# The 144-wide block's seven steps spread among a 656-wide block's in the pairwise-tanh stage, and the filter schedule shifted to match

## What is computed

```python
def _L2_attn_ref(B, W, v):
    Wi = jnp.einsum('bnd,ed->bne', B, W)
    scores = jnp.einsum('d,bijd->bij', v, jnp.tanh(Wi[:, None, :, :] + Wi[:, :, None, :]))
    attn = jax.nn.softmax(scores, axis=-1)
    return jnp.einsum('bij,bjd->bid', attn, B)
...
t = _to_tokens(x)
t = t + _L2_attn_ref(_ln_t(t), L2_attn_W, L2_attn_v)
t = t + _L2_ffn_ref(_ln_t(t), ...)      # 8 experts, the best 2 of each token
t = t + _L3_attn_ref(_ln_t(t), ...)     # causal linear attention
t = t + _L3_ffn_ref(_ln_t(t), ...)      # 16 spectral filters (causal convolutions), then mixing matrices
```

## Time and profile before

| | us |
|---|---|
| median of 3 runs | 12501.48 |
| lowest, highest | 12500.0, 12501.75 |
| the profiled execution | 12500.22 |
| its span, first to last instruction | 12498.5 |
| its mean granted TensorE clock | 0.98 |
| span's part before the first pass | 6203.7 |

### The profile page before, as it was taken

The page is one execution under the profiler, slowest core; times in us unless marked ns, Lnnn a source line. Parts: engine busy times, 40 slices in busy tenths (PEclk is TensorE's granted clock), DMA queues, the critical chain, the costliest instruction groups (busy, mean ns, idle before and its releaser), DMA issues. The chain is left out here.

```text
span 12498.5 us, 297675 instructions
## 1 busy us (share of the span) xinstructions
PE 11704.8 (94%) x123040; PEld 5806.2 (46%) x123040; DVE 11385.2 (91%) x21539; ACT 10886.1 (87%) x7444; POOL 126.2 (1%) x103
## 2 busy tenths in 40 slices
PE   8999999999999999999867999999999999999999
PEld 3333333333333333333323555555555555555567
DVE  9999999999999999999899888898888898989881
ACT  8999999999999999999788888888888888888872
POOL 0000000000000000000000000000000000000000
PEclk9999999999999999999978999999999999999999
DMA  0000000000000000000010111111111111111113
GB/s 14 2 7 2 4 4 2 7 2 4 4 2 7 2 4 4 2 4 2 23 45 1 50 52 51 53 53 50 50 52 52 52 54 49 50 52 53 50 57 108
DMA packets 290040, 355.08 MB, mean 28 GB/s; under 512 B 28040, under 2 KB 242960, under 8 KB 288656
## 3 DMA queue, kind: packets, MB, share of 16 engines
q1 hardware_dynamic: 288656, 335.48, 9.1%
HBM read 314.14 MB, written 21.23 MB: 27 GB/s over the span
## 5 line engine op out<-in xcount | busy, mean ns | idle before, releaser
L276 ACT ACTIVATE c_ring<-c_xn,c_w_neg 128x1568 f32<-128x1568 f32 x3824 | 5791.1, 1604 | 282.3 <-PE c_acc L235 275.5
L235 PE MATMUL c_acc<-c_ring,c_onehot 128*32 128x392 f32 x68608 | 5764.9, 493 | 138.3 <-DVE c_ring L434 79.3
L1101 ACT ACTIVATE t_ring<-t_ring 128x3120 f32<-128x3120 f32 (+56 forms) x2160 | 4498.7, 2111 | 913.9 <-DVE t_ring L1420 859.1
L426 DVE TENSOR_SCALAR c_ring<-c_xn,c_w 128x1568 f32<-128x1568 f32 x4752 | 4582.2, 1051 | 95.0 <-PE c_acc L235 95.0
L1420 DVE TENSOR_SCALAR t_ring<-t_proj 128x784 f32<-128x784 f32 (+63 forms) x10240 | 3907.2, 461 | 311.0 <-PE t_psS L1007 280.0
L235 PEld LDWEIGHTS c_acc<-c_ring,c_onehot 128*32 128x32 f32 x68608 | 2217.9, 110 | 3659.2 <-issue 3211.2
L1007 PE MATMUL t_psS<-t_ring,t_vhot 128*32 128x272 f32 (+22 forms) x36864 | 2375.6, 407 | 418.3 <-ACT t_ring L1101 242.4
L1007 PEld LDWEIGHTS t_psS<-t_ring,t_vhot 128*32 128x32 f32 x36864 | 1022.5, 113 | 1650.3 <-issue 992.7
L964 PE MATMUL t_psC<-t_filter_work 128*128 128x392 f32 (+3 forms) x6144 | 1663.9, 407 | 0.0
L964 PEld LDWEIGHTS t_psC<-t_filter_work 128*128 128x128 f32 x6144 | 1105.2, 191 | 689.2 <-issue 176.2
L434 DVE SCALAR_TENSOR_TENSOR c_ring<-c_xn,c_w,c_ring 128x784 f32<-128x784 f32 x1280 | 1275.6, 1047 | 95.8 <-ACT c_ring L276 94.6
(11 more groups left out here) (231 smaller groups left out, 3340.1 us busy)
## 6 DMA issues: line engine op xcount, KB each, us to landing
t_filter_work<-in_toep_dram SPq DMA_DIRECT2D x256, 393.0 KB, 3.3
t_filter_work<-mix_scratch SPq DMA_DIRECT2D x512, 192.0 KB, 2.5
t_filter_work<-in_toep_dram SPq DMA_DIRECT2D x256, 197.0 KB, 2.8
t_filter_work<-mix_scratch SPq DMA_DIRECT2D x512, 64.0 KB, 1.8
mix_scratch<-t_filter_work SPq DMA_DIRECT2D x4, 2048.0 KB, 9.5
c_xin<-in_x_dram SPq DMA_DIRECT2D x8, 784.0 KB, 4.4
x_scratch<-c_x1o SPq DMA_DIRECT2D x8, 784.0 KB, 3.4
t_proj<-x_scratch SPq DMA_DIRECT2D x16, 392.0 KB, 3.2
```

The lines of the kernel that those rows point to most:

```text
L235: mm = pe.matmul(acc[32 * g:32 * g + 32, ch, 0:HALF], onehot[:, 31 - r:63 - r], ring[:, s % RING, g, ch * HALF:(ch + 1) * HALF], start=(s ...
L276: ins = act.activation(tile4(ring[:, s % RING, g, :]), window(xn, tap), ACT.Relu, bias=w0_neg[:, tap, 4 * r + g:4 * r + g + 1])
L426: dve.tensor_scalar(tile4(ring[:, s % RING, g, :]), window(xn, tap), w0[:, tap, 4 * r + g:4 * r + g + 1], 0.0, ALU.subtract, ALU.max).then ...
L1101: act.activation(ring[:, st % RINGS, 0:n], ring[:, st % RINGS, 0:n], ACT.Tanh).then_inc(th.s, 1)
```

## The change

The order of blocks becomes 0, 4, 1, 5, 6, 3, 2. Block 5's seven steps don't follow one another: one stands behind every fourth step of block 1 (behind steps 3, 7, ... 27), and the corner stands directly behind the seventh. As block 5 now opens no accumulation of its own in its bank, its first matmul no longer starts one. Only blocks 0 to 4 wait for an evacuation, blocks 1, 5 and 6 are copied out together behind block 1's last step, and at the pass's end it is block 2 that is copied out in the next pass.

The batches keep their 34 places but the short one, with three steps, is now batch 21, at the end of block 1. Filter pairs 16 to 31 move one batch later, so batch 16 has none. Mixtures 16 to 29 follow one batch behind their filters as before, and the last two pairs of mixtures both stand in batch 33, the last of the pass. Some rows of the tables move by a step, and block 1's softmax and the next image's preparation by a batch.

```diff
-ORDER = [0, 4, 1, 3, 2, 5, 6]
+ORDER = [0, 4, 1, 5, 6, 3, 2]
...
-NS = START[6]
+SLOTS = []
+for _blk in (0, 4, 1, 3, 2):
+    for _k in range(STEPS[_blk]):
+        SLOTS.append((_blk, _k))
+        if _blk == 1 and _k % 4 == 3 and _k // 4 < STEPS[5]: SLOTS.append((5, _k // 4))
+NS = len(SLOTS)
+END = {blk: 1 + max(st for st, slot in enumerate(SLOTS) if slot[0] == blk) for blk in STEPS}
...
-BATCHES = {min(GROUP * B + GROUP - 1, NS - 1) for B in range((NS + GROUP - 1) // GROUP)}
+BATCH_AT = [4 * B + 3 if 4 * B + 3 < END[1] else 4 * B + 2 for B in range((NS + GROUP - 1) // GROUP)]
...
+def filters_in(j):
+    return j if j < 16 else j + 1
...
-          1: dict(fill=[batch(20, LATE), batch(21, EARLY)], filled=[84, 87], ...
+          1: dict(fill=[batch(21, LATE), batch(22, EARLY)], filled=[87, 90], ...
...
-AT_STU = dict(..., conv=[batch(u // 2, (FIRST, SECOND)[u % 2]) for u in range(64)], ...
-              mix=[batch(1 + m // 2, MIX) for m in range(64)], ...
+AT_STU = dict(..., conv=[batch(filters_in(u // 2), (FIRST, SECOND)[u % 2]) for u in range(64)],
...
+              mix=[batch(1 + filters_in(min(m // 2, 29)) if m // 2 < 30 else 33, MIX) for m in range(64)], ...
...
-                        if k == 0: W(pe, Sev, 0 if pos == 0 else scored(pos - 1), b)
+                        if k == 0 and blk < 5: W(pe, Sev, 0 if pos == 0 else scored(pos - 1), b)
...
-                                                    start=(r == 0), stop=(r == 31), skip_group_check=True)
+                                                    start=(r == 0 and blk != 5), stop=(r == 31), skip_group_check=True)
...
             def evacs(b):
-                for blk in ORDER[:5]:
-                    yield START[blk] + STEPS[blk] + AT_EVAC
+                for blk in ORDER[:-1]:
+                    yield END[min(blk, 1) if blk > 4 else blk] + AT_EVAC
                     evac(blk, b)
             def last_evacs(d):
                 yield -1
-                evac(5, d); evac(6, d)
+                evac(ORDER[-1], d)
```

More of the change, by code:

```diff
@@ L503, in step_rows @@
     return list(range(r0, min(r0 + PER_STEP[blk], 32)))
-SLOTS = [(blk, k) for blk in ORDER[:6] for k in range(STEPS[blk])]
-assert len(SLOTS) == NS and NS % RINGS == 0
+assert sorted(SLOTS) == [(blk, k) for blk in range(6) for k in range(STEPS[blk])] and NS % RINGS == 0
 SLOT = max(filled_at(*slot) for slot in SLOTS)
@@ L527 @@
 GROUP = 4
-BATCHES = {min(GROUP * B + GROUP - 1, NS - 1) for B in range((NS + GROUP - 1) // GROUP)}
+BATCH_AT = [4 * B + 3 if 4 * B + 3 < END[1] else 4 * B + 2 for B in range((NS + GROUP - 1) // GROUP)]
+assert BATCH_AT[-1] == NS - 1 and all(END[blk] - 1 in BATCH_AT for blk in range(5))
 def batch(B, rank):
-    return min(GROUP * B + GROUP - 1, NS - 1) + rank
+    return BATCH_AT[B] + rank
+def filters_in(j):
+    return j if j < 16 else j + 1
 FIRST, EARLY, MIX, LATE, SECOND = 0.0, 0.1, 0.3, 0.5, 0.8
@@ new lines @@
+AT_STU = dict(u=batch(32, EARLY), uev=130, res=batch(3, LATE), resev=16, conv=[batch(filters_in(u // 2), (FIRST, SECOND)[u % 2]) for u in range(64)],
+              conved=[int(batch(filters_in(u // 2), (0, 2)[u % 2])) for u in range(64)],
+              mix=[batch(1 + filters_in(min(m // 2, 29)) if m // 2 < 30 else 33, MIX) for m in range(64)], ar=[batch(1, EARLY), batch(17, EARLY)], out=[68, 1])
+AT_NEXT = dict(x=[batch(25, EARLY), batch(25, LATE)], tok=[102, 103], ln=dict(stats=104, aggr=106, norm=108), t=[batch(28, EARLY), batch(28, LATE)], tev=[114, 115],
+               w=[batch(29, EARLY), batch(29, LATE)], wev=[118, 119])
@@ L1007, in body @@
                                     ins = pe.matmul(psS[32 * q:32 * q + 32, at + lo:at + hi], vhot[:, 31 - r:63 - r], ring[:, st % RINGS, c + lo:c + hi],
[L1008 removed]
+                                                    start=(r == 0 and blk != 5), stop=(r == 31), skip_group_check=True)
                         ins.then_inc(s_credit, 1)
[L1010 to L1014 removed]
+                        if (blk, k) == (5, STEPS[5] - 1):
+                            W(pe, cth, 1, b)
+                            for r in range(TAIL):
+                                ins = pe.matmul(psS[0:32, CORNER_AT:CORNER_AT + TAIL], vhot[:, 31 - r:63 - r], corner[:, TAIL * r:TAIL * (r + 1)], start=False, stop=(r == TAIL - 1), skip_group_check=True)
+                            ins.then_inc(pK.s, 1)
+                        if st in BATCH_AT: step(st + 0.99)
                 run(tracks, body)
@@ L1179, in evac @@
                 wd = width(blk)[0]
[L1181 removed]
+                if blk < 5: dve.wait_ge(s_credit, NS * b + END[blk])
                 else: W(dve, pK, 1, b)
```

32 lines of the change are left out of this document (12 added, 20 removed).

## The result

| | before | changed |
|---|---|---|
| median, us | 12501.48 (7 runs, 12497.17 to 12503.79) | 12471.73 (7 runs, 12457.84 to 12474.27) |
| the profiled execution | 12500.22 | 12471.73 |
| its span | 12498.5 | 12469.9 |
| mean granted TensorE clock | 0.98 | 0.98 |

The ratio of the runs is 0.9972, with a 95% interval of 0.9963 to 0.9982. By the medians the change gains 29.8 us, or 0.24%. I had forecast 71 us. The sign and the range held, the size did not: 41 us are missing. The changed kernel's seven runs fall into two groups, three at 12458 to 12460 us and four at 12472 to 12474, and the profiled one is of the second. So a difference of less than 14 us from its 12472 says little.

A forecast was written before the change was run, and what follows sets the result against it. PE has the most work, 352.4 of 377.0 us a pass. Terms +0.3 +18.4 +2.3 -26.0 -0.7 gave -5.7, taken as -4.8; fourteen passes -67, with passes 0 and 1 -71: about 12430 us, range 12380 to 12505.

The forecast's parts named there:

- Stretch B: First half of block 1: DVE's longer sums for block 5 are hidden in its waits, +0.3 us a pass.
- Stretch C: Second half of block 1 until block 3 may start: seven more steps, 60.1 against 41.7 us, +18.4.
- Stretch D: Block 3: PE's first pair matmul waits 3.8 us for the values' copy; 51.2 against 48.9, +2.3.
- Stretches E and F: Block 2's first step to the next image's: PE's work moves ahead; 71.1 against 97.1 us, -26.0.
- The seam: Where a pass meets the next image's steps: PE waits 1.1 or 3.8 us, mean 2.4, instead of 6.39.
- Stretch A: Blocks 0 and 4: less of the first burst at the lower clock, -0.7 us a pass.
- Passes 0 and 1: Passes without filters, bounded by DVE: lose part of the seam's wait, about -2 us each.
- Tail: After the passes: two pairs of mixtures move inside PE's continuous work, 0 us, between -2 and +2.
- slack: Allowance for waits not found in the step-by-step sum, turning -5.7 into -4.8 us a pass.
- The first rival: Two more PE waits each followed by a lower-clock burst, 2.8 us together; -2.0 a pass, 12470 us, chance 0.13.
- My walk: DVE's and PE's work taken through the new order, each step starting when buffer and inputs are there; -5.7 a pass.
- The second rival: Waits only move: ten batches of block 1's end and block 3 each wait 0.45 more; 12493 us, chance 0.17.

The follow-up runs named there:

- e9: Changed kernel with six useless matmuls filling PE's wait for the values' copy in batch 24; 12415.16 us.
- e2: Changed kernel with the new order of steps alone, filters and mixtures not shifted; 12469.06 us.
- e3: Kernel before with only the shift of filters and mixtures, its order of steps kept; 12501.57 us.
- e10: e1 with eleven useless matmuls, five and six, in PE's two waits of batch 21; 12385.09 us.
- e12: e11 with ten useless matmuls, five ahead of the normalization's transposes and five behind the filter half in batch 21; 12385.16 us.
- e11: e1 with block 1's first transposes moved to batch 22, no matmul added; 12386.77 us.
- e4: Changed kernel with block 5's steps behind every fourth step of block 0 instead of block 1, block 0's softmax two batches later; 12491.61 us.
- e8: e1 with DVE's preparation of the next image one batch later; 12420.54 us.
- e1: Changed kernel with DVE's copy of the values one step earlier, behind the sums of step 101; 12400.35 us.
- e6: Changed kernel with DVE's copy of the values two steps earlier, behind the sums of step 100; 12432.72 us.
- e5: Changed kernel with twelve useless matmuls on PE ahead of the wait for the values' copy in batch 24; 12467.39 us.
- e7: e1 with fourteen useless matmuls, ten and four, in PE's two waits of batch 21; 12395.13 us.

## Why the prediction was right, and where it was wrong

- **Stretch B, +0.3**: right (0.0). The longer sums are hidden.
- **Stretch C, +18.4**: right to 0.1 us (+18.3), and that by luck. My 60.1 were 58.7 until block 1's copy lets PE go on, and 1.4 of work behind it at full clock. PE goes on after 57.3 already, in every pass, and the work behind takes 2.8 in nine of twelve passes (2.3 to 2.4 in the others), at the lower clock. At full clock C is 58.7, as in four passes of e9. DVE's part was 1.4 too long, and the slow burst that I had left out made up for it. The two waits were forecast as 2.6 and 4.3 and are 3.4 and 1.7, and the mixtures between them take 3.3 instead of 1.7.
- **Stretch D, +2.3**: the step that failed (+4.7). The chain was right: PE waits for the values' copy, 4.4 for my 3.8. But I let "13.1 until block 2 may begin" follow at full clock, and put the cost of a slow clock behind that wait at nothing. It took 15.3 (from 9417.49 to 9432.79), and 13.06 in e9. D is 51.0 in e9, where I had 51.2.
- **Stretches E and F, -26.0**: -25.1. The seam was even shorter than forecast (0.7 and 1.7 for my 1.1 and 3.8). That gain is given back in batches 26 and 27, which are 1.2 shorter in e9 at full clock. The 3.4 of mixtures at the seam were no gain of the pass, as e2 and e3 show.
- **Stretch A, -0.7**: wrong (+0.2). The clock rose as forecast, but ACT sets the first batch.
- **Passes 0 and 1, -4**: -9.8. DVE's idle time fell from 11.9 to 8.1 in pass 0 and from 14.2 to 9.9 in pass 1; I had taken part of one seam's wait. **Tail, 0**: pass 15 and the tail together are 2.6 longer, as far as one profile can tell.

Per pass the forecast was -4.8 and -1.9 was measured. Of the 2.9 between them D is 2.4, E with F 0.9 and A 0.9; B and C were 0.4 better, and 0.9 of slack was in the sum. With the wait of batch 24 filled (e9) the pass gains 6.1, more than I had forecast.

The first rival was what happened: slow bursts, 12470 and 0.13. Even its price was near (2.8 a pass, and 4.2 were measured). That its time fits to 2 us is luck in part: the slow clock cost more than it had, and the seam and DVE's part of C were shorter than my walk had them. It deserved more weight than the forecast. The evidence stood in the rows: 0.50 behind 6.39 of idle time and 0.93 in D behind 2.75. My walk had put waits of 2.6, 4.3 and 3.8 into each pass and had counted one slow burst. Against it I said that DVE is the bound in C and D. That holds for batch 21 (DVE busy 17.7 of 17.7), and nearly for 20 and 23, where both engines are busy almost throughout. It doesn't hold in batch 22, where PE is busy for all of the 11.2 and DVE for 9.5, nor behind the values' copy, where DVE itself idles (19.3 busy of 21.4 in batch 24) since it waits for the slow pair matmul. The second rival, waits that only move, holds for the filter shift alone. Between copy and pair matmul, the two engines wait for each other in turn, and a slow PE there is paid in full.

The kernels e10 to e12 beat both kernels: 12385 us, 0.9% less than before. e11 is the one to keep, as it has no useless matmuls.

What stays open: the changed kernel's runs fall into two groups 14 us apart, those of the kernel before lie within 7. Batch 21's lengths and those of D, 52.2 to 54.4 from pass to pass, could make that, but no run tested it, and no run of the faster group was profiled. Which waits are followed by the lower clock stays open too; that they were on the path is what e9 shows. Nor was the 2.6 us of pass 15 and the tail followed up.

## What to carry to other kernels

When a change leaves a new wait of several microseconds on TensorE, price the work behind it at the lower clock unless another engine is busy without a gap through that stretch; here that was 4.2 us a pass, more than the 3.7 by which the wait itself had grown (0.68 to 4.36). To tell a clock loss from a wait, fill the wait with matmuls that end just before it does, and size them from the trace. An engine's free time in one stretch says nothing of what moving work there will gain (e4, e8): compare the two sides batch by batch, there and where the work comes from, and look at what a moved piece will stand in front of. And a part of a sum that comes out right to 0.1 us can still hide two errors: check its pieces against the trace.

## What the runs showed of the hardware

- In the kernel before, each of the twelve seam waits of 3.7 to 6.5 us is followed by PE work at a granted clock of 0.50. In the changed kernel the wait of 4.36 lowers the clock of batch 24 to between 0.84 and 0.92 in all twelve passes (2.95 for 1.55 in the pass shown).
- The length of one wait does not settle it. One of 3.4 is followed by fast or slow transposes, in successive passes of one run. One of 1.69 leaves the clock at 1.00 in eleven of e1's twelve passes (0.91 in the last), while in e6 a wait of 1.69 in batch 25, with one of 0.39 behind it, goes with a clock of 0.89 to 0.91 in every pass.
- A wait of 1.21 in batch 26 is followed by a slow filter half (2.01 for 1.14) in nine of the changed kernel's twelve passes, and in none of e1's or e9's, where batch 24 is at full clock (but for one pass of e1). It isn't a rule: e5, e7, e11 and e12 have one such pass each with batch 24 at full clock.
- 12 matmuls of 128x384 in f32 stand as 24 in the trace and take 7.93 us, 0.66 for each one written.
